# Products of features: rows of four features with all six pairs among them, three copied factors a chunk instead of two, and two PSUM banks for fills and turns

## The reference

```python
e = stack([tbl_f[ids[:, f]] for f in range(39)], axis=1)      # 512 x 39 x 16
x0 = e; xi = e; res = []
for W in (W0, W1):                                            # 39*39 x 128, 39*128 x 128
    z = einsum('bmd,bnd->bdmn', x0, xi)                       # all products of features
    xi = einsum('bdp,po->bod', z.reshape(B, D, -1), W)
    res.append(xi)
z = concatenate(res, axis=1).sum(-1)                          # 512 x 256
h = concatenate([z, dense_ctx], axis=1)                       # 512 x 272
y = relu(relu(h @ W_top1 + b_top1) @ W_top2 + b_top2) @ W_top3
```

## Time and profile before

| | us |
|---|---|
| median of 3 runs (229.24 to 232.3) | 230.82 |
| profiled execution | 230.19 |
| its span, first to last instruction | 228.6 |
| busy: PE | 204.9 (90%) |
| busy: DVE | 176.5 (77%) |
| busy: ACT | 167.6 (73%) |
| busy: POOL | 109.2 (48%), all of it before 143 us |

### The profile page before, as it was taken

The page is one execution under the profiler, slowest core; times in us unless marked ns, Lnnn a source line. Parts: engine busy times, 40 slices in busy tenths (PEclk is TensorE's granted clock), DMA queues, the critical chain, the costliest instruction groups (busy, mean ns, idle before and its releaser), DMA issues.

```text
span 228.6 us, 4760 instructions
## 1 busy us (share of the span) xinstructions
PE 204.9 (90%) x1715; PEld 156.0 (68%) x1715; DVE 176.5 (77%) x295; ACT 167.6 (73%) x300; POOL 109.2 (48%) x106
## 2 busy tenths in 40 slices
PE   4577956879989998999999899799999999999995
PEld 4577813435556566777787577577778888889794
DVE  0899956999869899999979998798899787532010
ACT  6999465769867999798879998697867575775003
POOL 4788777777777777877777778000000000000000
PEclk9999779999999999999999999999999999999999
DMA  5950000240392591200240000003100000000000
GB/s 143 217 128 7 9 7 6 65 69 6 77 236 66 70 314 29 44 5 7 65 65 7 7 7 7 1 3 94 22 3 0 0 3 0 1 0 3 0 0 3
DMA packets 22015, 10.26 MB, mean 45 GB/s; under 512 B 11576, under 2 KB 20877, under 8 KB 21992
## 3 DMA queue, kind: packets, MB, share of 16 engines
q1 hardware_dynamic: 18728, 9.11, 16.4%
q0 software_dynamic: 3264, 0.84, 3.9%
HBM read 8.63 MB, written 1.31 MB: 44 GB/s over the span
## 4 chain that ended last, share of the span: by engine, by line
PE 60%; DVE 17%; ACT 9%; issue 7%; DMA 4%; POOL 1%; SPq 1%; DVEq 0%; ACTq 0%
PE s_bank L1013 14%; PE side_bank L967 6%; PE side_bank L969 6%; PE side_bank L968 6%; PE g_bank L995 4%; DVE z L786 3%; DVE z_lo L796 3%; DVE w_sb L725 3%; PE b_bank L947 3%; PE side_bank L962 3%; PE side_bank L995 3%; PE side_bank L934 3%; PE side_bank L975 2%; DMA feat<-tbl,ids_sb 2%; PE side_bank L912 2%
## 5 line engine op out<-in xcount | busy, mean ns | idle before, releaser
L387 POOL DMA_INDIRECT feat<-tbl,ids_sb x102 | 109.0, 1069 | 33.3 <-issue 21.9
L575 ACT ACTIVATE z_hi<-z 128x512 fp32r<-128x512 f32 x100 | 61.9, 632 | 10.6 <-DVE z L786 8.7
L786 DVE TENSOR_TENSOR z<-factors,b_bank 128x512 f32<-128x512 f32 x84 | 57.1, 681 | 7.9 <-PE b_bank L947 3.7
L796 DVE TENSOR_TENSOR z_lo<-z,z_hi 128x512 fp32r<-128x512 f32 x84 | 57.8, 688 | 0.3 <-ACT z_hi L575 0.2
L1013 PE MATMUL s_bank<-g,w_sb 128*128 128x128 f32 x312 | 47.5, 279 | 0.0
L1013 PEld LDWEIGHTS s_bank<-g,w_sb 128*128 128x128 f32 x312 | 44.1, 192 | 4.8 <-issue 2.4
L967 PE MATMUL side_bank<-z_hi,w_hi 128*128 128x512 f32 x84 | 42.3, 504 | 0.0
L969 PE MATMUL side_bank<-z_hi,w_lo 128*128 128x512 f32 x84 | 33.2, 396 | 0.0
L968 PE MATMUL side_bank<-z_lo,w_hi 128*128 128x512 f32 x84 | 32.9, 392 | 0.0
L467 ACT ACTIVATE factors<-side_bank 128x512 f32<-128x512 f32 x31 | 18.4, 594 | 7.2 <-PE side_bank L934 7.2
L947 PE MATMUL b_bank<-xs,sel 117*128 117x512 bf16 x48 | 18.7, 389 | 1.4 <-DVE direct_z L786 0.8
(11 more groups left out here) (181 smaller groups left out, 333.0 us busy)
## 6 DMA issues: line engine op xcount, KB each, us to landing
w_sb<-w SPq DMA_DIRECT2D x3, 832.0 KB, 5.8
feat<-tbl,ids_sb POOLq DMA_INDIRECT x102, 2.4
lines<-line SPq DMA_DIRECT2D x4, 320.0 KB, 2.2
diag<-lines SPq DMA_DIRECT2D x32, 40.0 KB
wt_sb<-wt SPq DMA_DIRECT2D x2, 512.0 KB
g<-small SPq DMA_DIRECT2D x1, 770.0 KB
g<-small SPq DMA_DIRECT2D x1, 448.0 KB
w0p<-w_pair SPq DMA_DIRECT2D x1, 448.0 KB
```

Of the source, the lines that this page charges most:

```text
L387: nc.gpsimd.indirect_dma_start(feat[:, bt % 2, n * D:(n + 1) * D], None, tables[order[n]], bass.IndirectOffsetOnAxis(ids_sb[:, bt, n:n + 1 ...
L575: nc.scalar.activation(z_hi[:, s % RING, :], z[:, at, :], ACT.Copy).then_inc(rounded, 1)
L786: nc.vector.tensor_tensor(target, one, other, ALU.mult).then_inc(product, 1)
L796: nc.vector.tensor_sub(low[rows, s % RING, :], z[rows, SPLITS[s] % Z_RING, :], z_hi[rows, s % RING, :].bitcast(f32)).then_inc(remainder, 1)
```

## The change

Each row has four features in place of five, and a row makes all six products among its four. Three of the four (a, b, c) are filled and copied to SBUF by ScalarE; one is selected and stays in PSUM. `ORDER` tells which two arrays each of the seven products takes; arrays 0 to 2 are the copied ones, 3 the selected one. There are rows of another layout of features (`FOURS`, `THREES`), which changes what the weights hold and not their number. The copied factors have a ring of two chunks (`F_RING`) of three in place of three of two.

```diff
-SELECTS = 3
-BASES = ((0, 5, 10, 13, 20), (0, 14, 3, 16, 21), (0, 8, 12, 14, 17))
+COPIES = "abc"
+ARRAYS = len(COPIES) + 1
+ORDER = ((0, 1), (0, 2), (1, 2), (0, 3), (1, 3), (2, 3), (0, 0))
+SELECT_AT = 1
-F_RING = 3
+F_RING = 2
-FILL_A = 4
-FILL_B = 3
+FILL_AT = (2, 3, 5)
-A_AT = [0, 24, 25, 25]
-B_AT = [0, 25, 26, 26]
+NEXT_FILL_AT = [(), (25, 26, 26), (25, 26, 26), (25, 26, 26)]
...
-        turn_banks = [turn_bank, g_banks[1], l1_bank[1], b_bank[1][:]]
+        turn_banks = [turn_bank, b_bank[1][:], g_banks[1], l1_bank[0], l1_bank[1]]
...
+        bank_of = {"a": 1, "b": 0, "c": 1}
...
-                        fills[0].append(("x", bt + 1, k))
+                        fills[k].append(("x", bt + 1, k))
...
-                for half, pair in enumerate((g_bank[:, :, :], side_bank[:, i % 2:i % 2 + 2, :])):
-                    act.wait_ge(g_summed, SETS * i + half + 1)
+                for half, pair in enumerate((side_bank[:, i % 2:i % 2 + 2, :], g_bank[:, :, :])):
+                    act.wait_ge(g_summed, SETS * i + min(half + 1, SETS))
...
-                k, j = u % 2, u // 2
-                if u < 2:
-                    dve.wait_ge(*after(turn_taken, "ab"[u], i, 0))
-                one = factors[:, i % F_RING, k, :]
-                if u == REST_T:
-                    other = one
-                else:
-                    dve.wait_ge(selected, SELECTS * i + j + 1)
-                    other = b_bank[(SELECTS * i + j) % B_RING][:]
+                for k, name in enumerate(COPIES):
+                    if u == max(k - 1, 0):
+                        dve.wait_ge(*after(turn_taken, name, i, 0))
+                if u == len(COPIES):
+                    dve.wait_ge(selected, i + 1)
+                one, other = (factors[:, i % F_RING, k, :] if k < len(COPIES) else b_bank[0][:] for k in ORDER[u])
...
-                    pe.wait_ge(g_copied, GPC * g_before_fill[n])
+                    pe.wait_ge(g_copied, GPC * g_before_fill[n] - 1)
...
-            def select(i, j):
+            def select(i):
 
-                q = SELECTS * i + j
-                if j == 0:
-                    features_there(i)
-                if q >= B_RING:
-                    before, number = divmod(q - B_RING, SELECTS)
-                    pe.wait_ge(product, PT * before + 2 * number + 2)
-                elif q == 1:
-                    pe.wait_ge(*after(turn_taken, "b", 0, 0))
-                nc.tensor.matmul(b_bank[q % B_RING][:], sel[:, j, :], columns(*divmod(i, CPT)),
+                features_there(i)
+                if i:
+                    pe.wait_ge(product, PT * (i - 1) + REST_T)
+                nc.tensor.matmul(b_bank[0][:], sel[:, ARRAYS - 1, :], columns(*divmod(i, CPT)),
```

More of the change, by code:

```diff
@@ L49 @@
 LAG = 5
-B_RING = 2
 DIRECT = [[1, 3, 5], [], [], []]
@@ L1205, in _factors @@
         for t in range(REST_T):
[L1206 to L1209 removed]
+            if max(ORDER[t]) < len(row):
+                item = tuple(sorted(row[k] for k in ORDER[t]))
+                if item not in seen:
+                    seen.add(item)
+                    pairs[t, p] = item
     for at in base_at:
```

140 lines of the change are left out of this document (77 added, 63 removed), and 3 rows, old and new, of the table FOURS.

## The result

The changed kernel took 238.55 us in the median of 4 runs (237.36 to 240.25), the kernel before 230.22 us (229.24 to 232.3, 4 runs on the same chip). The ratio is 1.035, with a 95% interval of 1.030 to 1.040. Each ratio in this document compares only those runs of a kernel that lie within 1.5% of its fastest. The prediction of 236.7 us, slower, holds, and the first thing to check is whether it holds for its reason. The profiled execution took 240.25 us, with a span of 238.7.

What follows compares the result with a forecast made beforehand. The prediction took GpSimd's serial gathers to bound the kernel until 144.2 us and TensorE after. From the profiled 230.19 us, +8.3 for held gathers, -1.15 for fewer matmuls and -0.6 for the turn gave 236.7 us; range 227.8 to 246.

Steps and rivals of the forecast that it cites:

- What bounds the kernel: Until 144.2 us GpSimd's back-to-back gathers, the last awaited 2.3 us by VectorE at step 77; then TensorE for 84.4 us.
- The term for the gathers: Before step 77, longer runs of two-SBUF-operand instructions hold gathers 0.75 us more a chunk, +8.3 us over 11 chunks.
- The rule under that term: A gather due inside a run waits 0.28 us, then passes each handover with chance 0.44 or waits 0.60 us more.
- The scale of 0.55: Factor on the rule's loss per chunk, as it gave 1.35 us for the kernel before where 0.75 was measured.
- +0 and +21.5 us: Bounds on the added gather loss: nothing if gathers keep in step with VectorE, +21.5 us if nothing falls into step.
- The upper end of the range: 246 us for the whole kernel, leaving out held-gather losses of over 2.25 us a chunk.
- 228.4: Rival before step 77: gathers keep in step, so only the 1.75 us gained after 144 us counts; 228.4 us, chance 0.20.
- TensorE's tail: From VectorE's going on after the last gather to the end: 82.6 us instead of 84.4, from savings of 1.15 and 0.6.
- Its part for the turn: Turn of tile 3 needs only the first of ScalarE's two copies of g: -0.6 us.
- The rest, -1.15 us for five matmuls: After 144 us TensorE has 4 selections and 12 fills instead of 13 and 8, five matmuls fewer: -1.15 us.
- The cover for ScalarE: 16 more copies, 9.5 us, cost 0: before 144 us covered by later gathers, after it by ScalarE's slack.
- The waits of VectorE: VectorE's wait for the last gather grows beyond 2.3 us, and a wait appears at steps 19 and 49.

Runs made afterwards that it cites:

- after2: The changed kernel unchanged, run again beside the kernel before on another chip: 237.91 us, ratio 1.029; profiled execution 236.98 us.
- b_sbuf3b: The kernel before with products u = 0, 1, 2 multiplying a copied factor by itself, both operands in SBUF: 240.05 us, ratio 1.040.
- a_mixed2: The changed kernel with its products reordered so PSUM products stand at u = 1, 3, 5, selection made earlier: 229.68 us, ratio 0.998.
- a_half: The changed kernel with every second gather of tiles 2 and 3 left out (30 of 102): median 228.81 us, ratio 0.977 by the first two runs.
- b_sbuf3: Same program as b_sbuf3b, on a chip where the kernel before took 254.5 us: 254.29 us, ratio 1.006.
- b_half: The kernel before with every second gather of tiles 2 and 3 left out, on a slow chip: 242.21 us, ratio 0.955.

## Why the prediction was right

The sum of 236.7 us was for a profiled execution. The two took 240.25 and 236.98. VectorE's row was foreseen at 152.5 (144.20 + 8.3) and came at 154.53 and 152.86; the tail was foreseen at 82.6 and took 84.2 and 82.5. So the first trace is off by 2.0 us in the gathers' part (1.3 in held time, 0.7 in a later first gather) and by 1.6 in the tail.

**What bounds the kernel** was right and is shown. VectorE waited for the last gather in all six traces of the table, its row follows the held time there, and where half of tile 2's and 3's gathers were left out the wait and the loss were gone. The margin can be thin, though: in after2 the last wait was 0.45 us. VectorE came to it at 152.41, where in the kernel before it came at 141.91, mostly because it had already waited 2.2, 4.9 and 2.8 us for gathers at steps 14, 19 and 70.

**The term for the gathers**, +8.3 us, was right in its cause and nearly in its size. Held time rose by 9.6 us in the first trace and by 8.5 in the second, VectorE's row came 10.3 and 8.7 us later, and the mean gather was 1176 and 1161 ns where I had said 1160. That one edit, operands in SBUF, carries it is shown by b_sbuf3b (1.040); that it is the place of these products and not their count is shown by a_mixed2 (0.998).

**The rule under that term** was worse than its result. It gave a held gather the same chance of 0.2 at every tight handover. Counted over the six traces in the table (the count takes every handover between two instructions with two SBUF operands at which a gather is waiting), some 96 of 155 got through where the instructions overlap, and all of some 60 where there is a break of 0.03 us or more between them. (Both totals move by a few with where one draws the edge of a handover.) Nor does it look like the same chance at each handover: most are through at the first one, and a few stay held past four or five, up to 4.00 us for one gather. Five gathers make 9.6 of the 16.7 us in the second trace. The scale of 0.55, fitted to the kernel before, absorbed this. Between +0 and +21.5 us it came within 1.3 us, and that is luck in part: a rule with a wrong chance in it has no claim to be so near. I would not trust it for a run of another length. The upper end of the range has a slip besides: 246 us belongs to a loss of 2.35 us a chunk (228.4 + 11 x 1.6), not of 2.25.

**What the Trainium skill says.** The Trainium skill, "SBUF — State Buffer", section "Who interferes with whom", says that a VectorE instruction with two SBUF inputs contends with a GpSimd instruction that reads SBUF, and b_sbuf3b bears that out (20.0 us held instead of 8.2). The inference in the same section of the Trainium skill, that `tensor_tensor` does not stall descriptor generation, is not borne out. A row of `tensor_tensor` shut out a gather for 3.06 us at 105.39, and without the term for the gathers the time would have been 228.4 us.

**TensorE's tail**, -1.75 us, was right where the clock held: 82.5 and 82.4 us in after2 and a_mixed2, against the 82.6 foreseen. Its part for the turn, -0.6 us, is shown by itself: the turn stands 2.55 to 2.57 us behind VectorE's row in the four traces with the changed banks and 3.14 in the two without. The rest, -1.15 us for five matmuls, is shown only in the sum. In the first trace the tail was 84.2, since TensorE was idle for 3.44 us there and the clock took 1.7 us. The prediction had no term for this. A later gather need not lengthen that idle time (it was 0.58 us in after2, 1.63 in the kernel before), since it depends on how much work TensorE still has; but the risk was there to be named.

**The cover for ScalarE** held. Waits for factor copies were 2.8 us in the products' group, against 3.3 before, and a_mixed2 has all 16 copies and takes 0.998.

**The waits of VectorE** were foreseen at steps 19 and 49 and behind the last gather. The first came, and longer than the gather was late:

```profile
65.44 0.26 DVE L708 TENSOR_TENSOR rest<-feat 128x96 f32<-128x96 f32 x1 [5.30 <-DMA feat<-tbl,ids_sb]
```

Its gather was issued 2.7 us later than in the kernel before and thereby into the transfer of two weight blocks of 832 KB, which keeps the DMA engines busy from about 61 to 68 us in both kernels; it landed 5.4 us after its issue instead of 2.4. This is the kind of collision that a late engine runs into. Behind it TensorE was idle for 5.79 us and its clock fell to the lower level there too (0.91 from 60 to 100 us), and VectorE took 22.1 us for the sixteen steps from 19 to 35, against 21.1 in the kernel before and 20.2 in a_half, where the clock stayed at full. None of this set the end, as the gathers ran on meanwhile with 0.30 us between two. At step 49 there was no wait; VectorE was by then itself 6.6 us later. Waits that the prediction did not name came at step 14 (1.06 us) and step 70 (2.18 us).

## What to carry to other kernels

Before moving an operand from PSUM to SBUF for VectorE, look at what GpSimd does beside it: if it issues indirect gathers back to back and something waits for the last, the place of such instructions in the order decides. Spread them among those that read PSUM, so that the runs in which a gather can be held stay short; here another order was worth 3% (1.029 against 0.998). It pays only where something waits for the gathers: on the chips of 254 us the long run cost nothing (1.006). And when a wait in front of TensorE grows, name the clock as a risk: in the tails, idle times of 2.35 and 3.44 us went with 1.5 and 1.6 us more, and one of 1.68 us with nothing.

## What the runs showed of the hardware

- All 173 gathers that were held over 0.1 us (seven traces) got in 0.11 to 0.14 us before the recorded end of a VectorE instruction with two SBUF operands; 65 of the 336 others did.
- A gather of 0.944 us got in at every one of some 60 handovers with a break of 0.03 us or more between two VectorE instructions that each read two SBUF operands, and at some 96 of 155 at which the two overlap by 0.08 to 0.09 us. What makes the difference among these is open.
- In step with gathers every second product takes 0.648 us from start to start instead of 0.602, so a gather costs VectorE 0.046 us there.
- At the turn of tile 3 TensorE's clock fell to its lower level behind an idle time of 3.44 us, at the end of one of 2.35 us, and behind 1.54 and 1.81 us with one matmul of 0.39 us between them; it stayed at full behind 1.63, 1.68 and 0.58 us. At step 19 it fell behind 5.1 to 5.8 us (four traces) and behind 2.12 us in a_mixed2, but in that same trace it stayed at full behind 2.30 us at 106.51. So the length of the last idle time does not settle it, and what else does is open.
- The same program took 230 us on some chips and 254 us on others, of which 13 us were in the look-up stage before the first product. On those the loss by the long run doesn't show (1.006 in b_sbuf3; the changed kernel as it is did not run there). A comparison of two kernels holds for the chip on which both ran.
- On those chips the traces have idle time that they put down to another core or an unknown queue, 17.3 us in b_sbuf3 and 4.2 in b_half, which has fewer gathers. Whether gathers bring it about was not tried.
